# A two-layer graph convolution with a final product: the second layer's weights applied to the gathered features, and each node's own row added by VectorE from its unsplit value

## What is computed

```python
def gcn_conv(x, W, b, src, dst, n):        # n = 6250 nodes, 200000 edges, 32 features
    h = x @ W
    s, d = concatenate([src, loops]), concatenate([dst, loops])
    deg = segment_sum(ones, d);  dis = rsqrt(deg)
    return segment_sum(h[s] * (dis[s] * dis[d])[:, None], d) + b

user_vec = user_emb[user_idx]                                  # 512 users
g = relu(gcn_conv(service_emb, W1, b1, src, dst, 6250))
g = gcn_conv(g, W2, b2, src, dst, 6250)
ctx = g[context_idx].reshape(512, 3 * 32)
return concatenate([user_vec, ctx], axis=1) @ fc_W + fc_b      # 512 x 6250
```

## Time and profile before

| | before |
|---|---|
| runs | 809.41, 814.43, 815.41 us; median 814.43 |
| profiled execution, first to last instruction | 789.6 us |
| PE busy | 599.2 us, 76% |
| DVE busy | 611.9 us, 77% |
| ACT busy | 411.9 us, 52% |
| chain that ended last | PE 52%, DVE 41% |
| DMA | 90.95 MB, mean 115 GB/s |

### The profile page before, as it was taken

How to read it: one execution, slowest core, us unless ns; L and a number is a source line. 1 busy time by engine, 2 the same in 40 slices (tenths; PEclk the granted TensorE clock), 3 DMA queues, 4 the chain that set the end, 5 groups by cost and what they waited for, 6 DMA issues and landing times.

```text
span 789.6 us, 21881 instructions
## 1 busy us (share of the span) xinstructions
PE 599.2 (76%) x9557; PEld 563.2 (71%) x9557; DVE 611.9 (77%) x1444; ACT 411.9 (52%) x700; POOL 131.8 (17%) x127
## 2 busy tenths in 40 slices
PE   0405652874674946257699999999999999999897
PEld 0305652774573936247699999999999999999643
DVE  8999999999999997987998888888886211111376
ACT  5892577697888511125568777777777400000000
POOL 0100000000000020047534444544300000000500
PEclk9999985977876975558989999999999999999999
DMA  7000000000000000022734555555300499958397
GB/s 125 2 0 1 2 1 0 1 2 1 1 1 1 2 4 1 0 69 50 240 128 176 179 190 191 191 181 177 134 4 2 180 415 405 367 184 297 97 315 291
DMA packets 37505, 90.95 MB, mean 115 GB/s; under 512 B 18246, under 2 KB 20989, under 8 KB 37406
## 3 DMA queue, kind: packets, MB, share of 16 engines
q1 hardware_dynamic: 25086, 74.69, 25.1%
q0 software_dynamic: 3648, 6.69, 4.5%
q10 hardware_dynamic: 8672, 8.13, 3.2%
HBM read 45.31 MB, written 44.18 MB: 113 GB/s over the span
## 4 chain that ended last, share of the span: by engine, by line
PE 52%; DVE 41%; ACT 2%; issue 2%; DMA 1%; POOL 0%; SPq 0%; DVEq 0%; POOLq 0%
PE pp L1348 17%; DVE arena L896 14%; DVE arena L897 13%; PE pp L1365 13%; PE psY L1365 12%; PE pp L1489 5%; DVE arena L883 2%; ACT arena L667 2%; PE pp L1286 1%; DVE arena L1070 1%; DVE arena L894 1%; DVE arena L891 1%; DVE arena L895 1%; DMA arena<-in_L_rec_edge_index_dram 1%; DVE arena L892 1%
## 5 line engine op out<-in xcount | busy, mean ns | idle before, releaser
L745 ACT ACTIVATE arena<-pp 128x512 uint16<-128x512 f32 x308 | 178.9, 585 | 69.4 <-PE pp L1348 64.0
L1348 PE MATMUL pp<-arena 128*128 128x128 fp8e4 (+1 forms) x2401 | 189.9, 221 | 8.6 <-DVE arena L1071 8.6
L667 ACT ACTIVATE arena<-arena,neg_word 128x780 fp8e4<-128x780 bf16 (+1 forms) x200 | 170.3, 945 | 2.1 <-PE psY L1267 2.1
L1348 PEld LDWEIGHTS pp<-arena 128*128 128x128 fp8e4 (+1 forms) x2401 | 150.4, 98 | 9.5 <-issue 8.2
L1365 PE MATMUL psY<-arena 128*128 128x96 bf16 x2401 | 150.3, 206 | 0.0
L611 POOL DMA_INDIRECT arena<-ordered_keys,window x98 | 111.0, 1133 | 163.2 <-PE pp L1348 92.7
L1267 PE MATMUL psY<-arena 128*128 128x128 fp8e4 x1563 | 109.8, 237 | 27.8 <-DVE arena L883 27.8
L1267 PEld LDWEIGHTS psY<-arena 128*128 128x128 fp8e4 x1563 | 109.4, 142 | 28.6 <-issue 26.9
L896 DVE TENSOR_TENSOR arena<-arena 128x832 f32<-128x832 f32 (+4 forms) x139 | 122.4, 880 | 3.8 <-ACT arena L690 0.2
L1365 PEld LDWEIGHTS psY<-arena 128*128 128x128 fp8e4 x2401 | 123.1, 98 | 0.0
L1070 DVE TENSOR_SCALAR arena<-arena 128x384 int32<-128x384 int32 (+5 forms) x224 | 107.0, 479 | 19.5 <-PE pp L1348 19.4
(11 more groups left out here) (193 smaller groups left out, 472.5 us busy)
## 6 DMA issues: line engine op xcount, KB each, us to landing
arena<-adjacency_spill SPq DMA_DIRECT2D x32, 784.0 KB, 9.6
adjacency_spill<-arena SPq DMA_DIRECT2D x24, 768.0 KB
adjacency_spill<-arena SPq DMA_DIRECT2D x8, 832.0 KB
out_dram<-arena SPq DMA_DIRECT2D x12, 512.0 KB, 3.6
out_dram<-arena ACTq DMA_DIRECT2D x8, 512.0 KB, 3.3
arena<-adjacency_spill SPq DMA_DIRECT2D x8, 392.0 KB, 4.6
arena<-in_L_rec_fc_W_dram SPq DMA_DIRECT2D x3, 784.0 KB, 6.2
arena<-in_L_rec_fc_b_dram SPq DMA_DIRECT2D x3, 784.0 KB, 6.8
```

The costliest lines, as they stand in the source:

```text
L667: ins = nc.scalar.activation(cols8[n % BUFS][:, 4 * u:4 * u + 4, 0:c1 - c0], high4[:, :, c0:c1], ACT.Sign, bias=neg_word[:, u:u + 1], satu ...
L745: nc.scalar.mul(adj16[g % SLOTS][:, m0 * P:m1 * P], bank(gp)[:, 0:(m1 - m0) * P], PAIR_SCALE).then_inc(evicted, 1)
L1348: ins = MM(bank(gp)[:, (n - n0) // 2 * P:((n - n0) // 2 + 1) * P], src_hot(h, n - a), dst_hot(h, n - a), start=n % 2 == 0, stop=n % 2 == 1 ...
```

## The change

Layer two's features are no longer multiplied with W2. `turn_x`, `copy_x` and `linear_x` go, with x_T and the semaphores between them, and `post_split` follows `post_sum` on DVE with a wait for x_set alone. `own_rows` goes on PE: in both layers DVE adds the own row with one scalar_tensor_tensor from X0, where the unsplit values now stay (the residues of layer one's split go to a buffer of their own, rest, and layer one's node values replace X0). In `to_table` the bias step goes, since bias 2 is now added behind W2. For each block of 128 batch rows the transposed features, with the three context parts ahead of the user part, are multiplied with W2 on PE (`weigh_features`) and get bias 2 on DVE (`mix_features`), ahead of the final product. For this the rows of fc_W are loaded in another order, in two transfers for each of its four pieces. The transposes of blocks 1 to 3 move from ahead of tile 9 to ahead of tile 8 of the block before, and the new product stands ahead of tile 10.

```diff
-TURN_AT = 9
+TURN_AT, MIX_AT = 8, 10
...
-        W2b = sb("W2b", [P, P], F32)
-        bias = sb("bias", [P, 2, D], F32)
+        W2b = sb("W2b", [CTX * D, CTX * D], F32)
+        bias = sb("bias", [P, D], F32)
+        bias2 = sb("bias2", [CTX * D, 1], F32)
...
+            sp.dma_start(bias[:], b1[None, :].to_broadcast((P, D))).then_inc(weights_in, 16)
+            for k in range(CTX):
                 sp.dma_start(W2b[k * D:(k + 1) * D, k * D:(k + 1) * D], W2).then_inc(weights_in, 16)
-            sp.dma_start(bias[:, 0, :], b1[None, :].to_broadcast((P, D))).then_inc(weights_in, 16)
-            sp.dma_start(bias[:, 1, :], b2[None, :].to_broadcast((P, D))).then_inc(weights_in, 16)
+                sp.dma_start(bias2[k * D:(k + 1) * D, :], b2.rearrange("(f o) -> f o", o=1)).then_inc(weights_in, 16)
...
-                    sp.dma_start(tile[:, c:c + w], whole[:, c:c + w]).then_inc(fc_in, 16)
+                    if what == 0:
+                        sp.dma_start(tile[0:CTX * D, c:c + w], whole[D:P, c:c + w]).then_inc(fc_in, 16)
+                        sp.dma_start(tile[CTX * D:P, c:c + w], whole[0:D, c:c + w]).then_inc(fc_in, 16)
+                    else:
+                        sp.dma_start(tile[:, c:c + w], whole[:, c:c + w]).then_inc(fc_in, 16)
...
-                    if g and k == turns_x(g)[1]:
-                        copy_x(g - 1)
...
-                    V.tensor_scalar(W2b[:], W2b[:], 1 / UNIT, None, ALU.mult)
...
-                V.tensor_tensor(X0, X0, parts[0][:, :, k - 1, :], ALU.subtract).then_inc(rest_ready, 1)
+                V.tensor_tensor(rest, X0 if k == 1 else rest, parts[0][:, :, k - 1, :], ALU.subtract).then_inc(rest_ready, 1)
...
+            def own(g):
+
+                return X0[:, first_chunk(g):first_chunk(g) + chunks_of(g), :]
...
-                return V.scalar_tensor_tensor(out=x, in0=x, scalar=0.0, in1=dis_w(c, w), op0=ALU.max, op1=ALU.mult)
+                return V.scalar_tensor_tensor(out=own(g), in0=x, scalar=0.0, in1=dis_w(c, w), op0=ALU.max, op1=ALU.mult)
...
                 link(V.tensor_reduce(x, thirds_of(y_s[:, g % 2, :], w), axis=AX.X, op=ALU.add))
+                link(V.scalar_tensor_tensor(out=x, in0=own(g), scalar=UNIT, in1=x, op0=ALU.mult, op1=ALU.add))
                 nodes_one(x, g, link).then_inc(x_set, 1)
...
             def post_split(g):
-                dve.wait_ge(z_done, g + 1)
-                split_z(g, link, xs[:, g % 2, 0:chunks_of(g), :]).then_inc(x_done, 1)
+                dve.wait_ge(x_set, g + 1)
+                split_x(g, link, xs[:, g % 2, 0:chunks_of(g), :]).then_inc(x_done, 1)
...
-                    to_table(i, g, x, link)
+                    link(V.scalar_tensor_tensor(out=x, in0=x, scalar=1 / UNIT, in1=own(g), op0=ALU.mult, op1=ALU.add))
+                    to_table(g, x)
...
+            def mix_features(b):
+
+                dve.wait_ge(feat_mixed, b + 1)
+                V.tensor_scalar(featT[0:CTX * D, b * P:(b + 1) * P], psX[0:CTX * D, b % 2 * P:(b % 2 + 1) * P], bias2[:, 0:1], None, ALU.add).then_inc(feat_ready, 1)
             copy_features(0)
-            dve.wait_ge(fc_in, 32 * -(-N // FC_PART))
+            mix_features(0)
+            dve.wait_ge(fc_in, 48 * -(-N // FC_PART))
...
-                if dd == 0 and g > 2:
-                    pe.wait_ge(x_done, g - 2)
...
-            def own_rows(tile, layer, g):
-                for dd in range(chunks_of(g)):
-                    ins = MM(tile[:, dd * D3:(dd + 1) * D3], identb[:], features(layer, first_chunk(g) + dd), start=False, stop=(dd == chunks_of(g) - 1))
-                return ins
...
-                    if g and k == turns_x(g)[0]:
-                        turn_x(g - 1)
-                    if g and k == turns_x(g)[2]:
-                        linear_x(g - 1)
...
+            def weigh_features(b):
+
+                pe.wait_ge(feat_copied, b + 1)
+                MM(psX[0:CTX * D, b % 2 * P:(b % 2 + 1) * P], W2b[:], featT[0:CTX * D, b * P:(b + 1) * P], start=True, stop=True).then_inc(feat_mixed, 1)
             pe.wait_ge(users_in, 16 * BB)
             turn_features(0)
-            pe.wait_ge(fc_in, 32 * -(-N // FC_PART))
+            weigh_features(0)
+            pe.wait_ge(fc_in, 48 * -(-N // FC_PART))
...
-                pe.wait_ge(feat_copied, b + 1)
+                pe.wait_ge(feat_ready, b + 1)
```

104 lines of the change are left out of this document (34 added, 70 removed).

## The result

| | before | after |
|---|---|---|
| median of 20 runs each, us | 810.02 (807.18 to 815.41) | 815.69 (811.08 to 818.72) |
| ratio | | 1.0054, 95% interval 1.0039 to 1.0068 |
| profiled execution, span | 789.6 us | 813.4 us |

The change makes the kernel 0.54% slower, 5.7 us by the medians, where 7.6 us less were forecast. It counts as same by the forecast's bound of 1%, but the time lies outside the range of 801.5 to 811.5 us. In the profiled execution of after the outside time is 815.16 us, so only 1.8 us lie around its span.

What follows compares the result with a forecast made beforehand. PE was taken to bound the kernel from about 400 us on. Removing 9.8 us and adding 0.4, 0.9 and 0.9 gave -7.6 us, from 814.43 to 806.8 us, range 801.5 to 811.5 us.

Steps and rivals of the forecast that it cites:

- The loads of the final product's weights: Ahead of the final product: eight transfers for four, issued at 713.04 us, used at 742.97, no one waiting; no cost.
- or if layer two's PE stops for loads: Layer two: a sign that would show the forecast wrong, PE stopping there for loads; no size or chance given.
- The groups of layer one: PE-bound layer one: PE loses 0.59 us in each of ten groups, 5.9 us; a group takes 19.86 us, not 20.45.
- DVE's wait a group: PE-bound layer one: VectorE's wait for PE falls from 1.95 to 1.0 us a group, so its added step stays hidden.
- Own rows and boundary: Layer two: 49 own-row matmuls go, 2.1 us; PE's stop for the last group's transpose at its start goes too.
- The second pair of legs ahead of the product: Between gathers and final product: W2 product 0.50 us and VectorE's bias step 0.44, adding 0.9 us.
- The final product: For the other three batch blocks, W2 products between PE-bound tiles add 3 x 0.29 = 0.9 us.
- VectorE with 12.7 us to spare in this stage: Final product: VectorE has slack to copy the features in time for each W2 product.
- The rival of the falling clock: Gap ahead of the final product: PE's clock falls to half for 5.7 us, costing 2.85 us, 809.7 us; chance 0.25.
- The first groups: Layer one ahead of 400 us: VectorE's added step delays two small one-hots PE waits for, costing 0.4 us.
- The level: Whole kernel: the 24.8 us between the 789.6 us span and 814.43 us median lie around the span, untouched.

Runs made afterwards that it cites:

- e9: The kernel before with only the output layer's weight loads divided into 96 and 32 partitions: 816.2 us, ratio 1.0056.
- e5: The changed kernel, unaltered, run and profiled again: 794.98 us, ratio 1.0037.
- e6: The changed kernel with the output layer's weights loaded whole again, users' rows in front and passed through an identity block in W2b: 789.47 us, ratio 0.9973.
- e1: The kernel before, unaltered, profiled once more: 810.33 us, ratio 1.0014.
- e12: The kernel before, unaltered, profiled in a later series: 812.59 us, ratio 1.0008.
- e13: The kernel of e6 (the changed kernel with whole loads) again, in another series: 811.27 us, ratio 1.0004.
- e2: Against the changed kernel, own rows stay on PE in both layers; W2 still behind the gathers, loads still divided: 810.25 us, ratio 1.0024.
- e7: The kernel before with 64 small useless products on PE ahead of layer one, which shift its later code: 791.54 us, ratio 1.0004.
- e8: The changed kernel with 64 small useless products on PE ahead of layer one, which shift its later code: 792.4 us, ratio 1.0013.
- e17: The kernel of e6 with each weight part loaded as two halves of 64 partitions: 796.53 us, ratio 1.0058.
- e18: The kernel of e16 again (against the changed kernel: whole loads, layer one's own rows on PE): 788.86 us, ratio 0.996.
- e11: The kernel of e6 with its weights in eight transfers of 128 partitions by half the columns: 810.4 us, ratio 0.9996.
- e16: The kernel of e2 with whole loads and the own rows on DVE in layer two only: 808.3 us, ratio 0.9971.

## Why the prediction was wrong, point by point

**The loads of the final product's weights: the step that failed.** "They are issued at 713.04 us and used at 742.97, so the 2 us that four issues take could double or triple with no one waiting." The issues were priced, and whether the data come in time. What the transfers do to others meanwhile was put at nothing. They hold the DMA engines for some 13 us instead of 8, at 60% of the rate, and PE stops twice, for 1.65 and 2.12 us in after. e9 prices this at 4.5 us by itself; e5 against e6 gives 5.5 us in the changed kernel, and after against e13, each by its ratio, 0.5% or 4 us. The forecast's last sentence, "or if layer two's PE stops for loads", names it, but no rival stood for it.

The profiles of e1 and after, both of the upper level, put the terms side by side. They are one execution each, 4.0 us apart where the medians are 5.7:

| | forecast, us | e1 to after, us |
|---|---|---|
| up to the first pick of group 3 | -0.1 | -1.6 |
| layer one from there | -6.1 | -1.3 |
| layer two, up to the transposition of block 0 | -3.2 | +2.2 |
| from there to the first product | +0.9 | +1.1 |
| the product and the end | +0.9 | +3.6 |
| sum | -7.6 | +4.0 |

The largest step is layer two, 5.4 us off, of which the divided loads make 4.2 us by e9's layer two. Layer one's missing gain is next with 4.8 us, then the clock in the product with 2.9.

**The groups of layer one.** At the level of the earlier trace rows the step was right: 19.92 us a group where 19.86 were forecast and 20.45 stood before, PE busy for all but 0.36 of 218.02 us, DVE's wait a group 1.07 us (1.0 forecast). From the first pick of group 3 on the layer is 224.42 - 218.02 = 6.4 us shorter. At the level at which the times were taken, the mean gain is only 1.3 us (table above). PE's work shrank by the forecast amount, and stops for nothing that the profile shows filled in.

**Layer two.** Own rows and boundary, 2.1 + 1.1 us of the forecast here: with whole loads 109.24 - 107.19 = 2.05 us at the lower level, 109.97 - 107.31 = 2.66 us at the upper (e12, e13). The own rows' 2.1 us fit that. The boundary's stop is gone, and most of its microsecond went to short stops shown as issue, 3.3 us in all in e6 against 2.5 in the earlier trace rows.

**The second pair of legs ahead of the product.** Forecast 0.9 us more than the earlier trace rows' 0.78: measured 1.67 to 1.71 us from the transposition to the first product (e5, e6, e13), right; 1.87 in after, at low clock.

**The final product.** Forecast 0.9 us for three W2 products. Each costs 0.22 us where the next block follows without a break, 10.86 instead of 10.63 us from one copy of DVE to the next (after, e1), so 0.7 us in all, and e2 has just that, 44.02 us. DVE wasn't in the way. Its additions start every 0.86 us, but the 0.17 us between them are waits for PE in the profile, and when it had fallen behind it did five in 3.26 us (the kernel before):

```profile
759.55 3.26 DVE L1227 TENSOR_TENSOR arena<-pp,arena 128x512 f32<-128x512 f32 x5 [0.18 <-DMA out_dram<-arena]
```

So "VectorE with 12.7 us to spare in this stage" was read rightly for the steady part. *The rival of the falling clock*, given 0.25, came true in after, and its price with it: 2.9 us forecast, 2.86 us measured. It came true at 1.7 us in e5 and e6. What nobody foresaw is DVE's pause at the upper level. It costs e13 a wait of 2.20 us, and 1.67 us for the clock that fell behind it (10.48 instead of 8.81 us for the same 22 matmuls). The cause of the pause is open. So is why the clock fell in some executions and stayed up in others: before itself has 43.34 us three times, 44.60 us in e12, by the pause, and 44.81 in e7, by the clock.

**The first groups.** Forecast 0.4 us lost. At the lower level the first pick of group 3 comes at 403.37, 401.52, 399.26 and 400.45 us (e5, e6, e8, e17) against 398.70 and 398.16 us in before and e7: 2.7 us later on the mean. e18, with PE's own rows, has 402.46, so DVE's added step is not shown to be the cause. At the upper level after has the pick at 409.90 and e1 at 411.50 us, no loss. What sets it stays open.

**The level.** 24.8 us between span and median were put down to what lies around. It is 1.8 us. The difference is the other level, in which PE has stops that my rows did not contain, so the sum was made on rows that don't hold for the runs it was meant for.

Put together at the lower level in the same way, e5's span against the earlier trace rows: +4.7 up to group 3's first pick, -6.4 in layer one, +2.4 in layer two (-2.05 and +4.4 for the loads), +0.1 to the transposition, +0.9 for the legs and +2.3 in the product, which is +3.9 us before rounding; the ratio of the series says 3 us (0.37%).

## What to carry to other kernels

A transfer that is in time can still cost: look at its rate and at who stops while it holds the DMA engines, and when a layout change tempts to divide a load by partitions, permute on TensorE instead, with a 128x128 matrix that costs what a 96x96 one costs. Take a second profile before building a sum on the first, and compare its outside time with the median it is to explain. When a stage comes out longer than its sum, time the same piece in several runs: eight tiles at 6.94 or 9.80 us told the clock's share from the rest. And a cut in an engine's work pays only as far as nothing fills the freed time: here PE lost 5.9 us of work in layer one and gained 4.6 us of idle time.

## What the runs showed of the hardware

- A load in pieces of 96 and 32 partitions, or of 64 and 64, moved 233 to 249 GB/s (e5, e9, e17), four whole loads 402 to 404 GB/s (e6, e12) and eight of all partitions 388 GB/s (e11), at a DMA share of 1.01 to 1.05.
- Where layer two's stream has no own rows in it, it breaks behind 127 or 128 matmuls or several times as many, for 0.2 to 1.1 us when the loads run at full rate (e6, e11, e13, e16) and up to 3.21 us when they are slow (e17). The profile calls this "issue". The stops measured end 2.3 to 2.9 us behind a packet of the DMA queue of kind "instruction". That they are late instructions is an inference that no run here proves.
- Eight tiles of the final product take 6.94 us at a granted clock of 1.00 (e2) and 9.80 us at 0.64 (after).
- The whole kernel has two levels 19 us (2.4%) apart, each for a whole series of runs; the same chip showed both. The cause is open.
